# Edge values of the first three row pairs: one fp32 product against three fp16 products with turned halves

## The reference

```
h  = relu(layernorm(x))
lQ, lK, lV = masked_x @ Wlq, h @ Wlk, h @ Wlv + blv
gs = (masked_x @ Wgq) @ (mean(h) @ Wgk).T / 16        # one score per row
es = masked_x @ Wes                                   # one score per row
eV = masked_x @ Wev + bev                             # the edge values
s  = where(adj, lQ @ lK.T / 16, -1e9)
m  = max(rowmax(s), gs, es);  le, ge, ee = exp(s - m), exp(gs - m), exp(es - m)
res = (le @ lV + ge * gV + ee * eV) / (sum(le) + ge + ee)
out = x + max(res, masked_x)
```

## Time and profile before

| | |
|---|---|
| median of 3 runs | 747.29 us (746.12 to 749.49) |
| the profiled execution's own time | 745.91 us |
| its span, first to last instruction | 744.1 us |
| PE busy | 721.6 us, 97% of the span |
| DVE, ACT, POOL busy | 561.1, 532.8, 443.8 us |
| granted TensorE clock, mean | 0.995 |

### The profile page before, as it was taken

One profiled execution on the slowest core, in us unless ns is written; L12 is line 12 of the kernel. 1 busy time (PEld: TensorE's weight loads), 2 busy tenths in 40 slices (PEclk: granted clock), 3 DMA queues, 4 the chain that ended last, 5 costly groups with the idle time before them and its releaser, 6 DMA issues. The chain is left out here.

```text
span 744.1 us, 14652 instructions
## 1 busy us (share of the span) xinstructions
PE 721.6 (97%) x5212; PEld 509.9 (69%) x5212; DVE 561.1 (75%) x1379; ACT 532.8 (72%) x701; POOL 443.8 (60%) x307
## 2 busy tenths in 40 slices
PE   7699999999999999999999999999999999999987
PEld 6366566666767777676767777676677777676776
DVE  5776677899677878778686778778686878677685
ACT  5783788666877777867877776868767776857690
POOL 2459579869566554655556554665556554653493
PEclk9899999999999999999999999999999999999999
DMA  7975277868898698897978898897978897968798
GB/s 205 234 190 102 55 159 151 185 127 172 182 176 174 138 212 152 160 178 160 194 151 175 142 209 157 168 169 166 185 151 178 137 217 150 172 139 181 131 190 151
DMA packets 366154, 123.20 MB, mean 166 GB/s; under 512 B 326272, under 2 KB 366080, under 8 KB 366080
## 3 DMA queue, kind: packets, MB, share of 16 engines
q1 hardware_dynamic: 366080, 122.26, 81.9%
HBM read 36.57 MB, written 4.19 MB: 55 GB/s over the span
## 5 line engine op out<-in xcount | busy, mean ns | idle before, releaser
L581 POOL TENSOR_TENSOR p_base<-s,p_base 128x1024 f16<-128x1024 f32 x108 | 232.3, 2154 | 229.5 <-ACT p_base L763 229.4
L995 PE MATMUL ps_u<-v_rows,pT_base 128*128 128x256 f16 x968 | 263.9, 273 | 3.2 <-DMA pT_base<-p_base 2.8
L997 PE MATMUL ps_u<-v_rows,pT_base 128*128 128x256 f16 x968 | 263.9, 273 | 0.0
L999 PE MATMUL ps_u<-v_rows,pT_base 128*128 128x256 f16 x968 | 263.9, 273 | 0.0
L734 ACT ACTIVATE bias<-adj,big 128x1024 f32<-128x1024 uint8 x128 | 157.8, 1237 | 118.3 <-DVE bmax L1320 109.2
L763 ACT ACTIVATE p_base<-s 128x1024 f16<-128x1024 f32 x122 | 129.0, 1057 | 42.5 <-DMA pT_base<-p_base 39.5
L747 ACT ACTIVATE s<-s,negm,invc 128x1024 f32<-128x1024 f32 x128 | 157.0, 1226 | 0.0
L995 PEld LDWEIGHTS ps_u<-v_rows,pT_base 128*128 128x128 f16 x968 | 94.7, 98 | 56.0 <-DMA pT_base<-p_base 3.3
L997 PEld LDWEIGHTS ps_u<-v_rows,pT_base 128*128 128x128 f16 x968 | 94.7, 98 | 52.1
L1320 DVE CUSTOM_DVE_ANT_0 s<-ps_x,bias 128x512 f32<-128x512 f32 x128 | 88.1, 689 | 46.2 <-PE ps_x L898 41.7
L999 PEld LDWEIGHTS ps_u<-v_rows,pT_base 128*128 128x128 f16 x968 | 94.7, 98 | 10.9
(11 more groups left out here) (217 smaller groups left out, 1272.1 us busy)
## 6 DMA issues: line engine op xcount, KB each, us to landing
adj<-adj SPq DMA_DIRECT2D x64, 256.0 KB, 3.5
s<-x SPq DMA_DIRECT2D x7, 512.0 KB, 5.0
f32q<-mx SPq DMA_DIRECT2D x14, 256.0 KB, 3.9
xm<-x SPq DMA_DIRECT2D x14, 256.0 KB, 3.5
xm<-mx SPq DMA_DIRECT2D x14, 256.0 KB, 4.0
out<-t_sb SPq DMA_DIRECT2D x14, 256.0 KB, 3.3
pT_base<-p_base SPq DMA_TRANSPOSE x120, 4.5
mxT_f<-mxT SPq DMA_DIRECT2D x4, 256.0 KB, 5.1
```

Source lines behind the costliest of these rows:

```text
L581: nc.gpsimd.tensor_tensor(p_rows(u)[:, 1], s32[:, p % NS, u % 2], p_rows(u)[:, 0], ALU.subtract).then_inc(s_plo, 1)
L995: nc.tensor.matmul(acc, turn[:, 0, j], v_rows[:, kc, 0:D], start=opens, stop=False, skip_group_check=True)
L997: nc.tensor.matmul(acc, turn[:, 0, j], v_rows[:, kc, D:2 * D], start=False, stop=False, skip_group_check=True)
L999: done = nc.tensor.matmul(acc, turn[:, 1, j], v_rows[:, kc, 0:D], start=False, stop=end, skip_group_check=True)
```

## The change

All pairs now take their edge values from the split product. For n = 0, 1, 2 the host-turned `mxT_f` is no longer loaded for this. Instead masked x of pair n is loaded by rows, scaled, halved and turned as for the later pairs, in between them: the order is pair 3, 0, 4, 1, 5, 2, 6, 7 and so on, and `rank(n)` is the place in that order. On DVE, ACT and POOL the new work stands in step 4n + 9, on SP the load in pass 4n + 8 and the transpose in pass 4n + 10. Because the buffers are shared, `q_high(n + 3)`, in step 4n + 10, now waits until the turned halves of pair n have landed.

```diff
+        def rank(n):
+            return 2 * n + 1 if n < QH else n - QH + min(n - QH, QH)
         def mx_home(n):
-            return mx_homes[(n - QH) % 4]
+            return mx_homes[3 if n < QH else (n - QH) % 4]
...
-            def load_mxT_f(n):
-                sp.wait_ge(s_side, 1)
-                if n >= 1:
+            def load_mx(n):
+                if n < QH:
+                    sp.wait_ge(s_mlo, rank(n))
+                else:
+                    sp.wait_ge(s_qlo, n - 1)
+                sp.dma_start(mx_rows, mx_pairs[n]).then_inc(s_mr, 16)
+            def transpose_mx(n):
+                sp.wait_ge(s_mlo, rank(n) + 1)
+                if n == 0:
+                    sp.wait_ge(s_side, 1)
+                elif n < QH:
                     sp.wait_ge(s_e, n)
...
                 if p % NG == 0 and QH <= (p + 4) // NG < NP:
                     transpose_mx((p + 4) // NG)
+                if p % NG == 0 and 0 <= p // NG - 2 < QH:
+                    load_mx(p // NG - 2)
+                if p % NG == 2 and 0 <= (p - 10) // NG < QH:
+                    transpose_mx((p - 10) // NG)
...
-                if p % NG == 0 and 0 <= p // NG - 2 < QH:
-                    load_mxT_f(p // NG - 2)
...
             def q_sums(n):
+                if QH <= n < 2 * QH:
+                    pool.wait_ge(s_mlo, rank(n - QH) + 1)
...
                 if p % NG == 3 and QH <= (p + 5) // NG < NP:
                     mx_low((p + 5) // NG)
+                if p % NG == 1 and 0 <= (p - 9) // NG < QH:
+                    mx_low((p - 9) // NG)
...
             def mx_high(n):
-                act.wait_ge(s_qT[(n - 1) % 2], ring(n - 1, 2))
+                if n < QH:
+                    act.wait_ge(s_mT, 16 * rank(n))
+                else:
+                    act.wait_ge(s_qT[(n - 1) % 2], ring(n - 1, 2))
...
                     act.wait_ge(s_qs, 4 * (n - PC // NG + 1))
+                    if QH <= n < 2 * QH:
+                        act.wait_ge(s_mT, 16 * (rank(n - QH) + 1))
                     nc.scalar.activation(q_hl[:, 0], f32q[:, 1:8], ACT.Copy).then_inc(s_qhi, 1)
...
                 if p % NG == 3 and QH <= (p + 5) // NG < NP:
                     mx_high((p + 5) // NG)
+                if p % NG == 1 and 0 <= (p - 9) // NG < QH:
+                    mx_high((p - 9) // NG)
...
             def es_values(n):
                 if n < QH:
-                    pe.wait_ge(s_mxf, 16 * (n + 1))
-                if n == QH:
+                    pe.wait_ge(s_mT, 16 * (rank(n) + 1))
+                if n == 0:
                     pe.wait_ge(s_wvlo, 1)
...
-                for t in range(2):
-                    for c in range(DC):
-                        last = nc.tensor.matmul(ps_q[:, t, 0:D], mxT_f[:, t, c], wev_sb[:, c], start=c == 0,
-                                                stop=c == DC - 1)
-                last.then_inc(s_e, 1)
+                split_product(n, wev_hl, D).then_inc(s_e, 1)
...
+                dve.wait_ge(s_w, n + 1)
+                if n < QH:
+                    dve.wait_ge(s_mu, rank(n) + 1)
+                nc.vector.tensor_tensor(wes[:, :], w3[:, :, 1], mu[:, n % 4, :, 1], ALU.mult).then_inc(s_wes, 1)
...
                     if project:
                         q_rows(m)
+                    if p == 9:
+                        mx_scale(0)
                     if low:
                         p_low(u + 1)
...
                     if step == 3 and (p + 5) // NG < NP and p >= 16:
                         mx_scale((p + 5) // NG)
+                    if step == 1 and p >= 16 and (p - 9) // NG < QH:
+                        mx_scale((p - 9) // NG)
...
                     if step == 3 and (p + 5) // NG < NP and p < 16:
                         mx_scale((p + 5) // NG)
+                    if p == 13:
+                        mx_scale(1)
```

More of the change, by code:

```diff
@@ L193, in build @@
             sem(n) for n in ("s_wqk", "s_wg", "s_wgv", "s_wlv", "s_wev", "s_bc"))
-        s_mxq, s_mxq1, s_mxf, s_xm, s_next, s_out = (
-            sem(n) for n in ("s_mxq", "s_mxq1", "s_mxf", "s_xm", "s_next", "s_out"))
+        s_mxq, s_mxq1, s_xm, s_next, s_out = (
+            sem(n) for n in ("s_mxq", "s_mxq1", "s_xm", "s_next", "s_out"))
         s_const = sem("s_const")
@@ L364, in load_mxT_q @@
                 sp.dma_start(mxT_q[:, :, :, :], mxT_pairs[n]).then_inc(s_mxq, 16)
-            def load_mxT_f(n):
-                sp.wait_ge(s_side, 1)
-                if n >= 1:
-                    sp.wait_ge(s_e, n)
-                sp.dma_start(mxT_f[:, :, :, :], mxT_pairs[n]).then_inc(s_mxf, 16)
             def load_mx(n):
-                sp.wait_ge(s_qlo, n - 1)
+                if n < QH:
+                    sp.wait_ge(s_mlo, rank(n))
+                else:
+                    sp.wait_ge(s_qlo, n - 1)
                 sp.dma_start(mx_rows, mx_pairs[n]).then_inc(s_mr, 16)
             def transpose_mx(n):
-                sp.wait_ge(s_mlo, n - QH + 1)
-                if n == QH:
+                sp.wait_ge(s_mlo, rank(n) + 1)
+                if n == 0:
+                    sp.wait_ge(s_side, 1)
+                elif n < QH:
+                    sp.wait_ge(s_e, n)
+                elif n == QH:
                     sp.wait_ge(s_q, QH)
@@ L561, in mx_low @@
             def mx_low(n):
-                pool.wait_ge(s_mhi, n - QH + 1)
+                pool.wait_ge(s_mhi, rank(n) + 1)
                 nc.gpsimd.tensor_tensor(mx_hl[:, :, 1], mx_rows, mx_hl[:, :, 0], ALU.subtract).then_inc(s_mlo, 1)
@@ L700, in mx_high @@
             def mx_high(n):
-                act.wait_ge(s_mscale, n - QH + 1)
-                act.wait_ge(s_qT[(n - 1) % 2], ring(n - 1, 2))
+                act.wait_ge(s_mscale, rank(n) + 1)
+                if n < QH:
+                    act.wait_ge(s_mT, 16 * rank(n))
+                else:
+                    act.wait_ge(s_qT[(n - 1) % 2], ring(n - 1, 2))
                 for t in range(2):
                     nc.scalar.activation(mx_rows[:, t], mx_rows[:, t], ACT.Copy, scale=mscale[:, t:t + 1]).then_inc(s_ms, 1)
-                act.wait_ge(s_ms, 2 * (n - QH + 1))
+                act.wait_ge(s_ms, 2 * (rank(n) + 1))
                 nc.scalar.activation(mx_hl[:, :, 0], mx_rows, ACT.Copy).then_inc(s_mhi, 1)
@@ L857, in project @@
                 else:
-                    pe.wait_ge(s_mT, 16 * (n - QH + 1))
+                    pe.wait_ge(s_mT, 16 * (rank(n) + 1))
                     if n == QH:
@@ L1005, in es_values @@
                 if n < QH:
-                    pe.wait_ge(s_mxf, 16 * (n + 1))
-                if n == QH:
+                    pe.wait_ge(s_mT, 16 * (rank(n) + 1))
+                if n == 0:
                     pe.wait_ge(s_wvlo, 1)
-                if n == 0:
-                    pe.wait_ge(s_wev, 16)
                 if n + 3 < NP:
@@ L1014, in es_values @@
                     pe.wait_ge(s_c2, 2 * n)
-                if n >= QH:
-                    split_product(n, wev_hl, D).then_inc(s_e, 1)
-                    return
-                for t in range(2):
-                    for c in range(DC):
-                        last = nc.tensor.matmul(ps_q[:, t, 0:D], mxT_f[:, t, c], wev_sb[:, c], start=c == 0,
-                                                stop=c == DC - 1)
-                last.then_inc(s_e, 1)
+                split_product(n, wev_hl, D).then_inc(s_e, 1)
             def es_values_end():
@@ L1216, in q_rows @@
                 if n >= QH:
-                    dve.wait_ge(s_mu, n - QH + 1)
+                    dve.wait_ge(s_mu, rank(n) + 1)
                     nc.vector.tensor_tensor(gs_es[:, n % 4], ps_q[:, :, D:D + 2],
@@ L1290, in mx_scale @@
             def mx_scale(n):
-                k = n - QH + 1
+                k = rank(n) + 1
                 dve.wait_ge(s_mr, 16 * k)
@@ L1400, in weights @@
                                         ).then_inc(s_w, 1)
-                if n >= QH:
-                    dve.wait_ge(s_w, n + 1)
-                    nc.vector.tensor_tensor(wes[:, :], w3[:, :, 1], mu[:, n % 4, :, 1], ALU.mult).then_inc(s_wes, 1)
+                dve.wait_ge(s_w, n + 1)
+                if n < QH:
+                    dve.wait_ge(s_mu, rank(n) + 1)
+                nc.vector.tensor_tensor(wes[:, :], w3[:, :, 1], mu[:, n % 4, :, 1], ALU.mult).then_inc(s_wes, 1)
             def side_rows(n, t):
@@ L1430, in es_rows @@
                 dve.wait_ge(s_e, n + 1)
-                if n >= QH:
-                    dve.wait_ge(s_wes, n - QH + 1)
+                dve.wait_ge(s_wes, n + 1)
                 for t in range(2):
                     dve.wait_ge(s_r, 4 * n + 2 * t + 2)
-                    scale = wes[:, t:t + 1] if n >= QH else w3[:, t, 1:2]
-                    nc.vector.scalar_tensor_tensor(r12[:, t], ps_q[:, t, 0:D], scale, r12[:, t], ALU.mult,
+                    nc.vector.scalar_tensor_tensor(r12[:, t], ps_q[:, t, 0:D], wes[:, t:t + 1], r12[:, t], ALU.mult,
```

(2 more changed lines are left out.)

## The result

The kernel after the change took 752.68 us (median of 5 runs, 750.59 to 753.73) against 746.12 us before (5 runs, 744.43 to 749.49). The ratio is 1.0085, 95% interval 1.0061 to 1.0109: slower by 6.3 us, by the two medians 6.6. The profiled execution took 750.88 us, 4.97 more than that of before. The forecast of 750.4 us with its range of 746.6 to 754.5 holds the time. But it lies above the likeliest case (749 to 752) and inside rival B's stretch (752 to 757): the forecast was +3.1 us, and twice that came.

The account below looks back on a forecast made before the run. The prediction took PE, busy for 97% of the span, to bound the kernel. Its terms, -0.85 + 3.0 + 1.3 + 0 = +3.4 us, stated as +3.1, took the median from 747.29 to 750.4 us, range 746.6 to 754.5.

Parts of the forecast that it names:

- likeliest case: The forecast itself, median 750.4 us: time between 749 and 752 us, chance 0.50.
- rival B: Stall spreads: shifted POOL meets DVE's tiny instructions elsewhere or a third PE wait; +6.5, 753.8 us (752 to 757), chance 0.19.
- PE's own work: es_values of pairs 0 to 2 each 0.43 us shorter; pair 0's lost in the wait before step 12; gain 0.85 us.
- DVE, step 9: mx_scale(0) between q_rows(3) and p_low(9) costs 0, as idle POOL frees DVE; bounds 0.3 us gained, 1.3 lost.
- POOL and ACT, step 9 to 10: mx_low(0) delays POOL's queue and q_high(3); PE waits in step 11, step 12 late: +3.0 us (+1.5 to +3.8).
- Step 13 to 15: mx_low(1) delays keys_t3(3) 3.2 us on POOL; PE waits for unit 18's transpose: +1.3 us (0 to +2.3).
- Step 17 to 20: q_high(5) waits 4.5 us on ACT for turned halves, 2.9 us to spare before step 20; cost 0, up to +1.0.
- a PE wait in steps 17 to 21: Sign against the forecast: PE waiting in these steps would show the prediction wrong.
- The sum: All terms: -0.85 + 3.0 + 1.3 + 0 = +3.4 us, stated as +3.1 because small slacks may take some.
- A: Waits of q_high(3) and p_low(18) mostly taken up as POOL catches up; +0.5, 747.8 us (746.8 to 749), chance 0.18.
- C: Faster: idle POOL removes contention in the DVE-bound stretch before steps 12 and 13; -3.8, 743.5 us, chance 0.04.
- D: No difference, everything hidden; only PE's -0.85 us remains, 746.4 us, chance 0.09.

Follow-up runs that it names:

- 1: Kernel before, with only es_values of pairs 0 to 2 as three fp16 products, taken from turned h, nothing prepared; ratio to before 0.9996.
- 3: Changed kernel with pair 0 prepared earlier: mx_scale(0) ahead of p_low(8), mx_high(0) right behind wev_high, transpose in SP's pass 9; ratio to before 1.0068.
- 5: Changed kernel with mx_low(0) behind keys_t4(3) on POOL in pass 9; ratio to before 1.0092.
- 6: Changed kernel with POOL's keys_t4(3) moved from pass 9 to pass 10, behind q_low(3); ratio to before 1.0102.
- 7: As 6, and SP issues the transpose of the halves of pairs 0 to 2 ahead of the mask load; ratio to before 1.0097.
- 4: Changed kernel with the halves of pairs 1 and 2 in their own memory (space of wev_sb), sparing q_high(4) and q_high(5) transpose waits; ratio to before 1.0103.
- 10: As 7, with key sums and differences of keys_t4(3) and keys_t3(0) on 4 of each 128 columns, results wrong; ratio to before 1.0023.
- 9: Kernel before, with only POOL's keys_t4(3) moved from pass 9 to pass 10, no work added; ratio to before 1.0022.
- 11: Changed kernel with the edits of 3 and 4 together; ratio to before 1.0058.
- 8: As 7, plus the own halves of 4, and keys_t3(3) moved to the end of POOL's pass 14; ratio to before 1.0086.

## Why the prediction was right, and where it was not

- **PE's own work, -0.85 us**: exact, by 1. It is also true that pair 0's share goes into the wait before step 12.
- **DVE, step 9, cost 0**: right. mx_scale(0) was free because POOL stood idle. 3 and 5 show the price when it does not: a PE wait of 1.4 to 1.8 us in step 10.
- **POOL and ACT, step 9 to 10, +3.0 us**: right in mechanism and size. mx_low(0) started at 133.25 (forecast 133.4), q_high(3) at 141.85 (141 to 142), PE's wait was 2.90 (2.8), step 12 at 159.50 (159.3): +3.26 from the mark. Missing was that DVE has a second limit just behind: 6 and 7 take the queue's wait away and get nothing back, since keys_t4(3) has to be somewhere, and beside DVE's rows before step 12 it costs the same.
- **Step 13 to 15, +1.3 us**: 1.7 measured, at es_values(1). POOL's delay is as forecast: p_low(18) starts at 190.73, 6.1 late with the 3.2 of step 12 in it. The wait behind it is another one. PE waits 0.16 for unit 18's transpose. Before that, DVE's out12(14) stood behind out11(14), which waited for p_low(18) to free its score buffer:

```profile
190.73 2.14 POOL L591 TENSOR_TENSOR p_base<-s,p_base 128x1024 f16<-128x1024 f32 x1
193.03 0.69 DVE L1330 CUSTOM_DVE_ANT_0 s<-ps_w,bias 128x512 f32<-128x512 f32 x1 [2.47 <-POOL p_base L591]
```

- **Step 17 to 20, "Cost 0", and step 16, for which the forecast has no term**: this is the step that failed. q_high(5) is released as forecast, by the turned halves, but waits 2.35 us for them and not 4.5, at no cost to PE (4). But two small waits cost 1.5 us, one in step 16 and one in step 17, and a PE wait in steps 17 to 21 was one of the forecast's own signs of being wrong. SP's load of the rows of pair 5 stood behind transpose_q(4), which came with the late q_high(4), so it went out at 196.93 instead of 190.62, the transpose of pair 5's masked x at 209.33 instead of 202.52, and project(5) waited 0.58 us for it. Then a pair of tiny DVE instructions met p_low on POOL:

```profile
218.53 2.13 DVE L1263 TENSOR_SCALAR big<-cq 128x2 f32<-128x2 f32 x2
...
218.40 2.16 POOL L591 TENSOR_TENSOR p_base<-s,p_base 128x1024 f16<-128x1024 f32 x1 [1.66 <-ACT p_base L780]
```

  Before, this pair took 0.24 us (at 213.33). It ended with POOL's instruction, and PE waited 0.53 at 221.38. So far rival B was right: meetings of 1 to 2 us elsewhere, and a third wait.
- **The sum**: counted from the mark, 3.26 + 1.67 + 0.76 + 0.73 for the waits, less 0.85, is 5.6 us in step 20, where +3.4 was forecast. (These waits cost some 0.2 us more than the brackets in their rows: 0.76 and 0.73 for 0.58 and 0.53.) The 1.5 us of steps 16 and 17 are two thirds of the difference. So the main mechanism was right and the size half of what came: that the time is inside the range is owed to the range, which took in half of B, and not to the sum. The profiles differ by 4.97 and the medians by 6.6. Why other executions lie above the profiled one, no trace shows. The mean granted clock does not put them in order: 0.993 at 750.59 and 750.88 us, 0.995 at 752.97, 0.991 at 753.73.
- **The other rivals**: A (taken up) fell, as POOL's gain of idle time came after q_high(3). C (faster) had its mechanism but not its size: without the added wait the thinned POOL of 10 brought step 12 forward by 0.7 us. D fell.

The Trainium skill (SBUF — State Buffer, Who interferes with whom) says that a DVE instruction with two SBUF inputs or in a two-port mode contends with a GpSimd instruction that reads SBUF, and the later one blocks. By that rule L1423, with two of its inputs in SBUF, should suffer from a POOL that is busy, and the traces agree: 1.20 us in 7, 0.48 in 10. Instructions on 128x2 elements with one input waited too (rclamp 1.02 us in 3); whether they are in such a mode, no run shows.

**Left open.** Five placements of pair 0's work gave step 12 at 45.7 to 47.7 us. A placement off this stretch altogether, before step 8, was not tried. Nor were pairs 1 and 2 taken apart, nor the added DMA traffic alone.

## What to carry to other kernels

Before adding work to a shared in-order queue, list what stands behind it and by how much each follower is early. Here 7.6 us of POOL's work stood behind one wait, with 1.0 us of slack. Where moving work inside a stretch only exchanges a queue's wait for contention, as in 6 and 7, the stretch has too much load in all, and less work is what helped (10; work moved out of the stretch was not tried): 0.85 us of PE's work was bought with work on four other queues in a stretch where DVE had none to spare. And look at the granted clock behind each long wait of PE.

## What the runs showed that I had not expected

- DVE beside a busy POOL: instructions of 0.17 us took 1.0 to 1.1 (3), a pair of 0.24 took 2.13 (after), L1423 and L1426 of 0.48 took 1.20 and 1.26 and p_low of 1.23 took 2.08 (7 against 10).
- Moving one block of POOL's work by one pass, with nothing added, cost 1.25 us (9).
- The granted clock fell to 0.50 behind PE waits of 2.23 (11), 2.31 (5), 2.37 (8), 2.65 (11), 2.89 (4), 2.90 (after) and 5.1 to 5.2 us (6, 7, 8), each time for some 3.4 us and in 6 for 6.8. It stayed at 1.00 behind waits of 2.23 (3), 2.56 (5) and 2.95 (9). So a wait can cost PE 1.7 us more than its own length (2.8 in 6), and a wait of the same 2.23 us before step 12 did so in kernel 11 and not in kernel 3. The kernels with the change fall into two groups: 54.0 to 54.3 us from step 12 to 16 where the clock held in that stretch, 55.5 to 56.8 where it fell.
- The kernel before has such a wait too, near its end: 2.83 us at 710.99, with the clock at 1.00 behind it. In 9 the wait at that place is 2.92 us (at 711.04), and there the clock fell to 0.50 from 711.0 to 714.3. So a fall of the clock may also be part of the spread between executions of the kernel before.
